# Attention in a two-network graph kernel: the products of a head with its values in one run behind the odd unit, none behind the even one

## The reference, cut to what matters

```python
q = (x @ wq + bq).reshape(N, H, Dh) * Dh ** (-0.5)      # N 1250, H 4, Dh 128
k = (x @ wk + bk).reshape(N, H, Dh)
v = (x @ wv + bv).reshape(N, H, Dh)
scores = einsum('ehd,ehd->eh', q[src], k[dst])
attn = softmax of scores over the edges of each src
out = segment_sum(attn[:, :, None] * v[dst], src)
x = x + (out.reshape(N, D) @ wo + bo)
```

## Time and profile before

| what | value |
|---|---|
| median of 2 runs (lowest, highest) | 1870.9 us (1869.83, 1871.98) |
| the profiled execution, its own time | 1871.84 us |
| its span, first to last instruction | 1870.1 us |
| PE busy | 1810.0 us (97%) |
| DVE busy | 1382.6 us (74%) |
| ACT busy | 826.5 us (44%) |
| POOL busy | 453.8 us (24%) |
| DMA, mean over the span | 58 GB/s |
| mean granted TensorE clock | 0.996 of full speed |

### The profile page before, as it was taken

One profiled execution on the slowest core, in us unless ns is written; L12 is line 12 of the kernel. 1 busy time (PEld: TensorE's weight loads), 2 busy tenths in 40 slices (PEclk: granted clock), 3 DMA queues, 4 the chain that ended last, 5 costly groups with the idle time before them and its releaser, 6 DMA issues. The chain is left out here.

```text
span 1870.1 us, 33910 instructions
## 1 busy us (share of the span) xinstructions
PE 1810.0 (97%) x11814; PEld 1575.5 (84%) x11814; DVE 1382.6 (74%) x2847; ACT 826.5 (44%) x1613; POOL 453.8 (24%) x547
## 2 busy tenths in 40 slices
PE   6988999999999999999999999999999999999999
PEld 4656988999789889998898899988998999887877
DVE  8996668888875588888754988888549888885431
ACT  1552465555432255554322545544226545536220
POOL 2000333112341341113413411125134111262000
PEclk9999999999999999999999999999999999999999
DMA  4213462110300111113011211040112110522001
GB/s 143 55 41 79 141 176 91 38 43 27 123 24 34 58 42 39 38 31 124 4 54 42 58 38 38 27 128 1 46 50 61 38 38 27 142 72 55 1 1 55
DMA packets 50755, 108.43 MB, mean 58 GB/s; under 512 B 18170, under 2 KB 18222, under 8 KB 50640
## 3 DMA queue, kind: packets, MB, share of 16 engines
q1 hardware_dynamic: 50608, 106.87, 19.7%
q0 software_dynamic: 32, 0.03, 0.0%
HBM read 83.62 MB, written 23.25 MB: 57 GB/s over the span
## 5 line engine op out<-in xcount | busy, mean ns | idle before, releaser
L876 ACT ACTIVATE PT<-ps 125x500 fp32r<-125x500 f32 (+1 forms) x480 | 214.3, 520 | 315.1 <-PE ps L1790 315.1
L1690 PE MATMUL ps<-PT,V 125*128 125x250 f32 x2400 | 313.2, 284 | 1.7 <-DVE PT L1288 1.7
L1690 PE MATMUL ps<-kT,qg 128*125 128x512 f32 (+1 forms) x1440 | 302.1, 354 | 6.3 <-DVE nmx L1272 5.6
L1690 PEld LDWEIGHTS ps<-kT,qg 128*125 128x125 f32 x1440 | 245.4, 186 | 56.0 <-issue 6.9
L1690 PEld LDWEIGHTS ps<-PT,V 125*128 125x128 f32 x2400 | 289.6, 190 | 2.9 <-DVE PT L1288 2.9
L1288 DVE TENSOR_TENSOR PT<-ps,PT 125x500 fp32r<-125x500 f32 (+1 forms) x480 | 253.1, 582 | 2.1 <-ACT PT L876 1.7
L1272 DVE CUSTOM_DVE_ANT_0 SB<-ps,bt 125x1250 f32<-125x1250 f32 x140 | 203.9, 1457 | 47.4 <-PE ps L1690 44.6
L1790 PE MATMUL ps<-ident,pbuf 125*125 125x125 f32 x1600 | 202.2, 273 | 9.9 <-DVE PT L1288 4.0
L1790 PEld LDWEIGHTS ps<-ident,pbuf 125*125 125x125 f32 x1600 | 187.2, 189 | 13.6 <-issue 8.8
L870 ACT ACTIVATE pbuf<-SB,nmx 125x1250 f32<-125x1250 f32 x140 | 188.1, 1344 | 12.1 <-DVE nmx L1272 10.4
L1281 DVE TENSOR_SCALAR pbuf<-pbuf,rden 125x1250 f32<-125x1250 f32 x160 | 150.1, 938 | 5.6
(11 more groups left out here) (246 smaller groups left out, 2811.6 us busy)
## 6 DMA issues: line engine op xcount, KB each, us to landing
bt<-edge_bias_scratch SPq DMA_DIRECT2D x40, 546.9 KB
q_scratch<-qc SPq DMA_DIRECT2D x16, 500.0 KB, 2.6
qc<-q_scratch SPq DMA_DIRECT2D x16, 500.0 KB, 4.8
counts_scratch<-cblk SPq DMA_DIRECT2D x10, 546.9 KB
c_rows<-counts_scratch SPq DMA_DIRECT2D x10, 546.9 KB
edge_bias_scratch<-b_rows SPq DMA_DIRECT2D x10, 546.9 KB
counts<-counts_scratch SPq DMA_DIRECT2D x10, 546.9 KB
wm<-in_L_gnn_wo_dram SPq DMA_DIRECT2D x4, 1024.0 KB, 8.6
```

The source lines that it names most:

```text
L876: sc.activation(PT[:, h % 2, 0, a:b, u * T:(u + 1) * T], ps_T[0:T, i, 0:(b - a) * T].rearrange("p (t n) -> p t n", n=T), ACT.Copy).then_in ...
L1690: e = mm(out_, lhs(a), rhs(b), start=start and i == 0, stop=stop and i == 2)
```

## The change

In `attn_rest` and `attn_end`, on PE alone, the two halves of a head become one block behind the odd unit, and the even unit is followed at once by the next unit's scores. No instruction is added or removed, apart from the waits of `attend`, which move with it. G0's head 0, whose first half stands ahead of unit 2, keeps its two halves; heads 3 and, in G4, head 2 were one block before.

```diff
                     else:
                         unit(G, k, False)
-                        attend(G, k // 2 - 1, k % 2)
+                        if begun and k == 3:
+                            attend(G, 0, 1)
+                        elif k % 2:
+                            attend(G, k // 2 - 1, 2)
 
             def attn_end(G, f, i):
                 for k in range(2, 6):
                     unit(G, k, True)
-                    attend(G, k // 2 - 1, k % 2)
+                    if k % 2:
+                        attend(G, k // 2 - 1, 2)
                 unit(G, 6, True)
                 attend(G, 2, 0)
                 attend(G, 2, 1)
```

## The result

The changed kernel took 1927.47 us (median of 2 runs, 1926.00 to 1928.95) against 1870.9 before: ratio 1.0303, 95% interval 1.0286 to 1.0320. It is slower, 3.5 us above the 1924 that was forecast and within the range. Two later series of five runs beside the kernel before gave 1.0302 (1.0287 to 1.0316) and 1.0310 (1.0296 to 1.0324), that is 57 and 58 us.

A forecast was written before the change was run, and what follows sets the result against it. PE was taken as the bound, without gaps in attention groups; new waits for the score maximum add 13.2 us per layer, about 53 in four layers, giving 1924 us (chance 0.80), range 1910 to 1940.

The forecast's parts named there:

- Where PE stands: Inside an attention group PE is busy 42.11 of 42.11 us, so any idle time the change gives it is paid in full.
- The chain: At even units the next scores wait for the maximum: 3.70 us (3.85 at first pairs) against 2.74 of PE work.
- The first link: From the start of scores to the start of their maximum on DVE: 2.10 us, 2.25 at a group's first unit.
- the second link: From the start of the maximum to the start of the scores it releases: 1.60 us.
- Nothing else late: DVE and ACT keep up in the new pair; the narrowest place, the odd turning's copies, has 0.4 us to spare.
- Rival 1: DVE slides out of step, so odd turnings or maxima come late: 0.33 us more per pair, 1941; chance 0.08.
- The sum: Per layer: first pairs of G1 to G4 4.5, heads 1 and 2 of G0 to G3 7.8, G0 0.4, G4 0.5 us.
- The last group: G4's second pair: moved products delay unit 6's turning by some 1.6 us, of which about 0.5 reach the end.
- Rival 2: PE's clock falls to half at each new wait, up to 1.9 us more per pair: 2023; chance 0.02.
- the old one of 1.32 us: A PE wait in attention of the kernel before, after which the clock was 1.00; new waits were said to be shorter.
- Rivals 3 and 4: 3: wait at the next scores is covered, near 1868, chance 0.07; 4: half the cost comes back later, 1897, 0.03.

The follow-up runs named there:

- The fillers: Six extra, overwritten products at each of the 52 even units: changed kernel with them 1923.19 us (ratio 1.0283), kernel before with them 1907.09 us (1.0200).
- the run with the filler: Changed kernel plus six extra, overwritten products behind unit 4 of each layer's last group only: 1922.85 us.
- The splits: Kernel before with heads divided unequally at the 52 places: three tiles behind the even unit, seven behind the odd, 1873.82 us; one and nine, 1904.57 us.
- the split of one and nine: Kernel before with one tile (three products) behind the even unit and nine behind the odd one at the 52 places: 1904.57 us, ratio 1.0185.
- the mirror: Kernel before with all thirty products behind the even unit and none behind the odd one at the same places: 1918.90 us, ratio 1.0259.
- the split of three and seven: Kernel before with three tiles (nine products) behind the even unit and seven behind the odd one at the 52 places: 1873.82 us, ratio 1.0023.

## Why the prediction was right, point by point

**Where PE stands.** That PE has no idle time in a group and that all of a new wait is paid: right. The fillers show it from both sides (+37 us in the kernel before, nothing in the changed one).

**The chain.** Forecast 2.10 (2.25) + 1.60 = 3.70 (3.85) us; measured 3.63 (3.77), and 3.73 for head 2. The first link was exact for heads 0 and 1; the second was 0.08 too long. The trace does not put that down to the length of the wait: the second link is 1.52 us at every new wait of G1 to G3 (waits of 0.65 to 0.82 us) and 1.60 to 1.62 in G0 and G4, behind waits of 0.14 as well as of 1.90 us. The earlier trace rows are from G0. G1 to G3 are the groups in PE's loop, and G0 and G4 stand outside it; whether that is the reason was not tried. Head 2's first link is 783.09 - 780.88 = 2.21 us, for which I have no reason. Pairs: 10.09 and 10.24 foreseen, 10.03 to 10.19 measured; the group +3.1 foreseen, +3.0 measured.

**Nothing else late.** Right: DVE waits for PE ahead of each even maximum; the odd turnings follow their scores after 1.81 us with no wait (766.24 - 764.43). Rival 1 did not come.

**The sum.** Forecast 53 us, measured in the trace 52.1 without the falls of the clock. The middle groups came out at +3.0 where 3.1 was forecast, and the first pair of G4 at 10.09 us (860.95 - 850.86 in layer 1) instead of 10.24. G0 came out at +2.1, +2.7, +2.8 and +2.8 us where 2 x 0.97 + 0.37 = 2.3 was forecast, since the maximum of unit 6 starts 2.6 to 3.0 us after its scores there, where the one row had 2.47. These misses have both signs, and that they nearly cancel is luck, though a small one.

**The last group.** The 1.6 us that were to shrink to 0.5 shrank to 0.38: 876.83 - 860.95 = 15.88 us in layer 1, against 15.50 before. But the step behind it missed something. I had scores 7 at the same moment as before and did not read this as what it is for PE, a wait of 1.90 us, more than twice the length of most others.

**Rival 2, the clock.** I gave it 0.02 and priced it for all pairs or none. It comes at one kind of place only, behind the wait of 1.90 us, in three layers of four, and costs 4.4 us by the run with the filler. The other 52 waits, most of them 0.65 to 0.85 us and the longest 1.6 us (in G0, where DVE is late), left the clock at 1.00. This is the term that was missing from the sum: 53 us foreseen, 57 and 58 measured in the two later series, and 53.7 (1922.85 - 1869.14) with the falls prevented. That the new waits are shorter than the old one of 1.32 us, as the prediction put it, was wrong for these four and for two of the four in G0 (1.60 and 1.59 us). The Trainium skill (TensorE: Matmul & The Clock Gate, "A second HAM failure mode: psum-queue depth-cycling") has the direction right, that brief idling between groups of matmuls can lower the clock. The trace agrees at the longest wait (1.90 us) and disagrees at all the shorter ones, which come every 10 us in a group, at a clock of 1.00.

**Rivals 3 and 4.** The splits have as many joins as the kernel before, and one of them still costs 34 us; no cost came back later, apart from the 1.2 us a layer in the last group that the sum had counted on.

## What to carry to other kernels

Where an engine is full, what stands between two of its dependent steps is cover: add up the chain through the other engines (here 3.7 us) and keep at least that much independent work between them, start to start. Beyond it the placement is nearly free: nine products or fifteen behind the even unit differ by 0.2%, three or none by 2 to 3%. And look for the one place where the same edit opens a longer gap than elsewhere, since the clock may take its own price there.

## What the hardware showed that I had not expected

A wait of 1.90 us made the granted clock fall from 1.00 to 0.50 in three of four last groups in each of three profiles of the changed kernel, though not always in the same layers, and cost 1.6 us each time. Putting 0.7 us of useless matmuls into it (1.21 us of idle time are left) prevented that and made the kernel 4.4 us faster. At the same place a wait of 1.55 us, behind three products (the split of one and nine), left the clock at 1.00 in all four layers, and so did the mirror's wait of 1.74 us between two turnings.

Length alone does not decide. The same 1.90 us left the clock at 1.00 in one layer of four each time. At the start of layer 0's attention, code that the change does not touch, PE waits for 2.04 us in the kernel before and in the second profile of the changed one:

```profile
274.11 1.32 PE L1790 MATMUL ps<-ident,pbuf 125*125 125x125 f32 x10 [2.04 <-DVE PT L1288]
...
274.25 2.41 PE L1790 MATMUL ps<-ident,pbuf 125*125 125x125 f32 x10 [2.04 <-DVE PT L1288]
```

Behind the first the clock is 1.00, behind the second 0.50, and the ten turnings take 2.06 us to the start of the next block instead of 1.37. One block earlier PE was idle for 1.27 us in the first and 1.68 us in the second, but that does not decide either: with 1.26 and 2.04 us the clock fell in the profile of the split of three and seven. What does decide was not tried. Nor does a fall always cost time: in this second case the turnings and the scores behind them took 1.3 us longer, but in the third profile of the changed kernel the clock fell one block earlier, behind idle time of 2.00 us there, and PE's next wait for DVE was 1.3 us shorter (0.73 instead of 2.04), so that nothing was lost.
